# Rows of C for a selective scan: broadcast by DMA through DRAM instead of by matmul and copy

## The chip, the cores and the metric

The kernel runs on one core of one Trainium2 chip. The metric is the time of one execution on the device, in microseconds (us), as the median of several runs.

## The reference

Four layers follow one another on a tensor of 4 images x 64 x 64 pixels x 128 channels. Layers 0, 1 and 3 are vision state space layers, layer 2 is a gated block without a scan. What matters here is the scan of layers 0, 1 and 3, cut to its core:

```
xs = stack([x0, x1, x0 reversed, x1 reversed])   # 4 directions, 256 channels, 4096 positions
dts, Bs, Cs = split(x_proj @ xs, [8, 16, 16])    # per direction
delta = softplus(dt_w @ dts + dt_b)
h = exp(delta * A) * h + (delta * x) * B         # state: 256 channels x 16
y = sum over the 16 states of h * C
```

x1 is x0 with rows and columns of the image exchanged. After the scans the four directions are summed, normalized, multiplied by a gate silu(z), projected, and an MLP with gelu follows. Each layer also has a layernorm and (in the scan layers) a depthwise 3x3 convolution ahead of it.

## The kernel before

**Tiling.** Channels lie on the 128 partitions, 256 channels make two halves h (DH = 2). The 4096 positions are cut into 8 chunks of 512 (CH, NCH). For each of 12 images (3 scan layers x 4) the function `scans` runs the four directions in the order DIRS = (0, 2, 1, 3), and in each the 8 chunks: the first and the last are written out, the six between are three passes of a loop over two chunks. A chunk has N = 16 steps, one for each state n. So there are 12 x 4 x 8 = 384 chunks and 6144 steps, and each step does its work on both halves.

**One step, engine by engine.** Every engine has its own `chunk` function, and all order comes from semaphores.

- TensorE spreads row n of B over the 128 partitions by a bf16 matmul with a selector SEL (`spread`, L349), two steps ahead, into one of two PSUM banks BB. It spreads row n of C the same way, one step ahead, into the one bank CB. It also sums the products h * C of step n - 4 into the PSUM banks YB with a matmul by the identity (`sum_states`, L361; LAG = 4).
- ScalarE copies CB to the readout ring CS in SBUF (L780; RING = 4 slots), computes the decay factors exp(delta * A) of both halves into two PSUM banks DAB (L787), and saves the last column of the state of the step before into CARRY (`save`, L767).
- VectorE multiplies delta * x by B (L567) and runs the recurrence (L584, a tensor_tensor_scan that reads the decay from PSUM), once for each half. The states go to the ring HS (4 slots).
- GpSimd multiplies the state by C (L937), from HS and CS to the ring HC (4 slots).

**Between chunks.** The next chunk is prepared in slots of the present one: PE_SLOTS, ACT_SLOTS, DVE_SLOTS and POOL_SLOTS name the step after which each piece runs. The projection of the next chunk gives a tile RAW (L739) whose rows 0 to 15 are B, 16 to 31 are C and 32 to 39 the step sizes; it is split into three bf16 parts in PARTS. At step MERGE = 4 ScalarE takes the finished sums of the chunk before out of YB (`take_sums`, L771). In directions 1 and 3 (o = 1) it writes them with rows and columns exchanged. TensorE's first `sum_states` of the new chunk waits for it.

**DMA.** The SP queue issues all transfers. In a scan layer it stores the gates silu(z) to DRAM, reads them back into X0 after the second direction (L280), loads the residual after the last chunk (L260), and stores the results. DIAG, the diagonals of the convolution, is a view of the same memory as CS, and TensorE reads it (L428) until the fifth tile of the convolution is done.

Of the kernel before, what the change touches and what calls it, by code (L numbers as in the profile page):

```python
# [34 lines left out]
LAG = 4  # L35

# [45 lines left out]
def program(nc, x_in, consts, sel_in, w0, w1, wg, w3, out):  # L82
    ctx = ExitStack()
    with ctx:
# [9 lines left out]
        gates = nc.dram_tensor("gates", [P, DH, L], F32).ap()  # L94
        sources = [x_in, *hidden]
# [8 lines left out]
        SEL = sb("SEL", [P, 2 * N, P], BF16)  # L104
# [36 lines left out]
        YB, DAB, BB, CB, PB = PS[:, 0:2], PS[:, 2:4], PS[:, 4:6], PS[:, 6], PS[:, 7]  # L141
# [17 lines left out]
        def both(ap):  # L159
# [13 lines left out]
            "b_ready", "c_ready", "decay_ready", "c_copied", "input_ready", "state_ready", "carry_ready",  # L173
# [25 lines left out]
        class Chunk:  # L199


            def __init__(self, img, ki, j):
# [6 lines left out]
                self.turned = img.scan(NCH) + NCH  # L209

# [42 lines left out]
        def _(sp):  # L253
            sp.dma_start(KC[:, :], consts).then_inc(s["consts_loaded"], 16)
            sp.dma_start(SEL[:, :, :], sel_in).then_inc(s["consts_loaded"], 16)
            for layer, (kind, weights, _) in enumerate(layers):
# [10 lines left out]
                def image(b, more):  # L267
# [5 lines left out]
                    else:  # L273
                        for t in range(NCH):
                            sp.wait_ge(s["gate_ready"], img.scan(NCH) + (t + 1))
                            sp.dma_start(gates[:, :, tok(t)], SZT[t % 2]).then_inc(s[f"gate_stored{t % 2}"], 16)
                        for q in range(2):
                            sp.wait_ge(s[f"gate_stored{q}"], (img.scan(NCH // 2) + NCH // 2) * 16)
                        sp.wait_ge(s["y_merged"], img.scan(CHUNKS) + 2 * NCH)
                        sp.dma_start(X0[:, :, :], gates).then_inc(s["gates_loaded"], 16)  # L280
                        sp.wait_ge(s["y_merged"], img.scan(CHUNKS) + CHUNKS)
# [23 lines left out]
        def _(pe):  # L305
# [58 lines left out]
            def chunk(c, prev, nxt, par):  # L364
                for n in range(N):
# [7 lines left out]
                    if n + 1 < N or nxt:  # L373
                        pe.wait_ge(s["c_copied"], st + 1)
                        m = (n + 1) % N
                        spread(CB, N + m, par if n + 1 < N else 1 - par).then_inc(s["c_ready"], 1)
# [15 lines left out]
            for layer, (kind, _, _) in enumerate(layers):  # L392
# [3 lines left out]
                with pe.Fori(0, NB) as b:  # L396
# [4 lines left out]
                    if kind == "scan":  # L401
# [40 lines left out]
                        spread(CB, N, 0).then_inc(s["c_ready"], 1)  # L442
# [95 lines left out]
        def _(dve):  # L538
# [30 lines left out]
            def chunk(c, prev, nxt, par):  # L569
                for n in range(N):  # L570
                    st = c.step + n
                    for h in range(DH):
# [11 lines left out]
                        dve.tensor_tensor_scan(c.run(HS[n % RING][:, h]), c.run(DAB[:, h]), c.run(DBX[n % 2][:, h]),  # L584
# [137 lines left out]
        def _(act):  # L722
# [12 lines left out]
            def prepare(i, par, op, first=False):  # L735

                if op == "raw":
                    act.wait_ge(s["proj_ready"], i + 1)
                    act.activation(RAW[:, :], PB, ACT.Identity, bias=col(K_ROW)).then_inc(s["raw_ready"], 1)  # L739
# [33 lines left out]
            def chunk(c, prev, nxt, par):  # L773
                final = nxt is None or nxt.k != c.k
                for n in range(N):
                    st = c.step + n
                    act.wait_ge(s["c_ready"], st + 1)
                    if prev or n >= RING:
                        act.wait_ge(s["readout_ready"], st - (RING - 1))
# [253 lines left out]
```

## Time and profile before

| | |
|---|---|
| median of 3 runs | 26486.41 us (26484.9 to 26491.68) |
| span of the profiled execution, first to last instruction | 26472.5 us |
| what the median has around that span | 13.9 us |
| VectorE busy | 25249.3 us, 95% |
| TensorE matmul busy | 20800.8 us, 79% |
| GpSimd busy | 16821.7 us, 64% |
| ScalarE busy | 16551.4 us, 63% |
| mean DMA traffic | 8 GB/s |
| mean granted TensorE clock | 0.957 |

A page of the profile lists busy time by engine and by line. Times of single instructions overlap a little where one starts before the write of the last has ended, so the interval from start to start is what a step costs. Idle time of an engine is put down to what released it.

### The profile page before, as it was taken

To read this page: it belongs to the slowest core of one execution; us is meant where nothing else is said; L and a number is where in the kernel's file an instruction comes from. 1 tells how busy PE (TensorE), PEld (TensorE's weight loads), DVE (VectorE), ACT (ScalarE), POOL (GpSimd) and SP (SyncE) were. 2 spreads that over 40 slices of the span, in tenths; PEclk is the share of its full clock that TensorE was granted. 3 is DMA by queue.
4 is the path that set the end of the run, shared out by engine and by line. 5 is a ranking of instruction groups with operands and counts; after the bars stand their busy time and mean duration, and the time that the engine had idled before them with its cause. 6 is when DMAs were issued, how large, how long until landed. Compare 5 with 4: busy or idle time off the path is not lost.

```text
span 26472.5 us, 271753 instructions
## 1 busy us (share of the span) xinstructions
PE 20800.8 (79%) x48516; PEld 8224.1 (31%) x49344; DVE 25249.3 (95%) x28655; ACT 16551.4 (63%) x31677; POOL 16821.7 (64%) x7108
## 2 busy tenths in 40 slices
PE   7778778778777777877877877787778778778777
PEld 3333333333333333333333333333333333333333
DVE  9998998998999899899899899969999998998998
ACT  6665665665666566666566566656666665665665
POOL 5765765775677477577577567707775765775775
PEclk9999999999999999999999999999999999999999
DMA  0000000000000000000000000010000000000000
GB/s 15 7 0 17 7 0 16 0 7 16 1 7 4 16 7 1 16 0 7 16 0 7 10 7 7 0 58 1 7 4 13 7 0 16 0 7 16 1 7 7
DMA packets 53095, 222.41 MB, mean 8 GB/s; under 512 B 4384, under 2 KB 4512, under 8 KB 45600
## 3 DMA queue, kind: packets, MB, share of 16 engines
q1 hardware_dynamic: 51744, 209.22, 2.1%
q14 instruction: 1091, 8.94, 0.1%
q8 instruction: 260, 4.26, 0.1%
HBM read 125.31 MB, written 83.89 MB: 8 GB/s over the span
## 4 chain that ended last, share of the span: by engine, by line
issue 48%; DVE 34%; PE 7%; ACT 7%; DVEq 3%; POOL 0%; DMA 0%; ACTq 0%; another core or an unknown queue 0%; POOLq 0%; SPq 0%
DVE WK L584 21%; DVE WK L567 7%; PE PS L361 3%; DVE WK L561 2%; ACT PS L787 2%; DVE WK L558 2%; PE PS L474 1%; PE PS L487 1%; ACT YP L771 1%; DVEq L577 1%; DVEq L579 1%; DVE X L645 1%; ACT CS L780 1%; ACT WK L762 1%; PE PS L349 1%
## 5 line engine op out<-in xcount | busy, mean ns | idle before, releaser
L937 POOL TENSOR_TENSOR HC<-WK,CS 128x1024 f32<-128x1024 f32 x6144 | 14824.7, 2415 | 7065.8 <-DVE WK L584 5702.7
L584 DVE TENSOR_TENSOR_SCAN WK<-PS,CARRY,WK 128x512 f32<-128x512 f32 x12288 | 15593.2, 1269 | 114.0 <-ACT PS L787 99.5
L787 ACT ACTIVATE PS<-WK,ANEG 128x512 f32<-128x512 f32 x12288 | 8452.0, 691 | 8013.6 <-DVE WK L584 8009.6
L361 PE MATMUL PS<-HC,KC 128*128 128x512 f32 x24576 | 12368.4, 628 | 648.9 <-ACT YP L771 641.3
L567 DVE TENSOR_TENSOR WK<-WK,PS 128x512 f32<-128x512 f32 x12288 | 8055.4, 656 | 46.6 <-DVE WK L584 45.0
L349 PE MATMUL PS<-PARTS,SEL 128*128 128x512 bf16 x11616 | 3727.7, 398 | 4715.8 <-DVE WK L567 4560.8
L361 PEld LDWEIGHTS PS<-HC,KC 128*128 128x128 f32 x24576 | 4849.4, 200 | 5367.6 <-issue 3879.4
L349 PEld LDWEIGHTS PS<-PARTS,SEL 128*128 128x128 bf16 x12288 | 1155.0, 99 | 9761.2 <-DVE WK L567 8332.6
L780 ACT ACTIVATE CS<-PS 128x512 f32<-128x512 f32 x6144 | 3586.9, 584 | 379.2 <-PE PS L349 358.4
L924 POOL TENSOR_TENSOR WK<-WK 128x1024 f32<-128x1024 f32 x384 | 911.4, 2373 | 2416.4 <-DVE WK L555 2416.4
L767 ACT ACTIVATE CARRY<-WK 128x2 f32<-128x2 f32 x5376 | 1012.8, 188 | 0.0
L928 POOL TENSOR_TENSOR WK<-WK 128x1024 f32<-128x1024 f32 x384 | 909.7, 2369 | 1.8
L345 PE MATMUL PS<-RAW,W 9*128 9x512 f32 x1536 | 874.3, 649 | 12.3
L357 PE MATMUL PS<-YP,KC 128*128 (+1 forms) x1152 | 870.2, 884 | 0.0
L645 DVE SCALAR_TENSOR_TENSOR X<-YP,W,X 128x512 f32<-128x512 f32 x1056 | 755.8, 790 | 0.0
L319 PE MATMUL PS<-X,W 128*128 (+1 forms) x1536 | 751.1, 612 | 0.0
L684 DVE SCALAR_TENSOR_TENSOR WK<-PS,W,X 128x512 f32<-128x512 f32 x96 | 72.0, 750 | 570.7 <-PE PS L474 570.7
L561 DVE TENSOR_TENSOR WK<-WK,X 128x1024 f32<-128x1024 f32 x384 | 604.3, 1574 | 0.4
L771 ACT ACTIVATE YP<-PS 128x1024 f32 (+1 forms) x384 | 560.0, 1458 | 70.4 <-PE PS L361 70.4
L754 ACT ACTIVATE WK<-PS 128x512 f32<-128x512 f32 x768 | 444.0, 578 | 76.3 <-PE PS L345 76.3
L555 DVE TENSOR_SCALAR WK<-WK 128x1024 f32<-128x1024 f32 x384 | 489.4, 1275 | 0.0
L428 PE MATMUL PS<-YP,CS 128*128 128x512 f32 x1080 | 477.8, 594 | 0.6
(114 smaller groups left out, 11580.2 us busy)
## 6 DMA issues: line engine op xcount, KB each, us to landing
gates<-WK SPq DMA_DIRECT2D x96, 512.0 KB, 3.0
X<-gates SPq DMA_DIRECT2D x12, 4096.0 KB, 12.8
X<-hidden SPq DMA_DIRECT2D x20, 2048.0 KB, 8.0
hidden<-WK SPq DMA_DIRECT2D x96, 256.0 KB, 2.0
X<-in_x SPq DMA_DIRECT2D x8, 2048.0 KB, 8.8
YP<-hidden SPq DMA_DIRECT2D x4, 2048.0 KB, 9.2
out<-WK SPq DMA_DIRECT2D x32, 256.0 KB, 2.0
W<-w SPq DMA_DIRECT2D x3, 2004.5 KB, 12.4
```

The costliest lines, as they stand in the source:

```text
L349: return pe.matmul(bank, SEL[:, row], PARTS[:, parity], start=True, stop=True)
L361: mm = pe.matmul(YB[:, h], ident, HC[:, slot, h], start=(n == 0), stop=(n == N - 1))
L561: dve.tensor_tensor(DX[par], DELTA[par], nxt.X[:, :, nxt.tokens()], ALU.mult).then_inc(s["dx_ready"], 1)
L567: dve.tensor_tensor(DBX[slot][:, h], DX[par][:, h], BB[:, slot], ALU.mult).then_inc(s["input_ready"], 1)
L584: dve.tensor_tensor_scan(c.run(HS[n % RING][:, h]), c.run(DAB[:, h]), c.run(DBX[n % 2][:, h]), CARRY[:, n, h:h + 1], ALU.mult, ALU.add).th ...
L645: ins = dve.scalar_tensor_tensor(conv, window, w, conv, ALU.mult, ALU.add)
L767: act.activation(CARRY[:, n], source, ACT.Copy).then_inc(s["carry_ready"], 1)
L780: act.activation(CS[:, n % RING], CB, ACT.Copy).then_inc(s["c_copied"], 1)
L787: act.activation(DAB[:, h], DELTA[par][:, h], ACT.Exp, scale=ANEG[:, a:a + 1])\
L924: pool.tensor_tensor(ROUND[par], EXPV, ROUND[par], ALU.subtract).then_inc(s["err_ready"], 1)
L928: pool.tensor_tensor(LOGV, LOGV, ROUND[par], ALU.add).then_inc(s["log1p_ready"], 1)
L937: pool.tensor_tensor(HC[:, n % RING], HS[n % RING], both(CS[:, n % RING]), ALU.mult).then_inc(s["readout_ready"], 1)
```

## The change

C no longer passes through TensorE and ScalarE. Once a chunk's RAW is there, SP stores its rows 16 to 31 to DRAM, eight copies of each (`store_c`). For each step SP loads row n from the eight copies, each read sixteen times, onto the 128 partitions of a slot of CS (`load_c`, 256 KB). The load waits until GpSimd has done the product that last read the slot; the load of step 15 waits for one product more and so speaks for the load of the next chunk's step 0 as well. The store of the next chunk's rows is placed behind the load of step 5. For the first chunk of an image the store waits until the convolution on TensorE has ended, since CS and DIAG share memory.

The PSUM bank that held C becomes a third bank for decay factors, so that ScalarE can be three half steps ahead of VectorE's scan instead of two. The carry is saved two steps late instead of one (SAVE). The selector has half its rows, and the gates are read back into X0 after the last chunk instead of after the second direction, just ahead of the residual's load.

```
+REPS = 8
+SAVE = 2
+STORE = 5
+DECAY_BANKS = (2, 3, 6)
+        c_rows = nc.dram_tensor("c_rows", [2, REPS, N, CH], F32).ap()
-        SEL = sb("SEL", [P, 2 * N, P], BF16)
+        SEL = sb("SEL", [P, N, P], BF16)
-        YB, DAB, BB, CB, PB = PS[:, 0:2], PS[:, 2:4], PS[:, 4:6], PS[:, 6], PS[:, 7]
+        YB, BB, PB = PS[:, 0:2], PS[:, 4:6], PS[:, 7]
+            def c_loads(self, n):
+                return (self.i * (N // RING) + n // RING) * 16
+            def decay_bank(self, n, h):
+                return PS[:, DECAY_BANKS[(DH * n + h) % len(DECAY_BANKS)]]
...
+            def store_c(par):
+                sp.dma_start(c_rows[par].rearrange("r n l -> n r l"),
+                             RAW[N:2 * N, :].rearrange("p (o l) -> p o l", o=1).to_broadcast([N, REPS, CH]))\
+                  .then_inc(s["c_stored"], 16)
+            def load_c(c, n, par):
+                rows = c_rows[par, :, n:n + 1, :].to_broadcast([REPS, P // REPS, CH])
+                sp.dma_start(CS[:, n % RING], rows).then_inc(s[f"c_loaded{n % RING}"], 16)
+            def chunk(c, prev, nxt, par):
+                for n in range(N):
+                    st = c.step + n
+                    if n == 0:
+                        sp.wait_ge(s["c_stored"], (c.i + 1) * 16)
+                    elif prev or n >= RING:
+                        sp.wait_ge(s["readout_ready"], st - (RING - 1) + (nxt is not None and n == N - 1))
+                    load_c(c, n, par)
+                    if nxt and n == STORE:
+                        sp.wait_ge(s["raw_ready"], nxt.i + 1)
+                        store_c(1 - par)
...
+                        sp.wait_ge(s["conv0_ready"], img.scan(CONV_PE) + CONV_PE)
+                        store_c(0)
+                        scans(sp, img, chunk)
                         for q in range(2):
                             sp.wait_ge(s[f"gate_stored{q}"], (img.scan(NCH // 2) + NCH // 2) * 16)
-                        sp.wait_ge(s["y_merged"], img.scan(CHUNKS) + 2 * NCH)
+                        sp.wait_ge(s["y_merged"], img.scan(CHUNKS) + CHUNKS)
                         sp.dma_start(X0[:, :, :], gates).then_inc(s["gates_loaded"], 16)
-                        sp.wait_ge(s["y_merged"], img.scan(CHUNKS) + CHUNKS)
                         load(src, b, XI, "residual_loaded")
...
-                    if n + 1 < N or nxt:
-                        pe.wait_ge(s["c_copied"], st + 1)
-                        m = (n + 1) % N
-                        spread(CB, N + m, par if n + 1 < N else 1 - par).then_inc(s["c_ready"], 1)
...
                 if op == "raw":
                     act.wait_ge(s["proj_ready"], i + 1)
+                    if not first:
+                        act.wait_ge(s["c_stored"], i * 16)
...
-                    act.wait_ge(s["c_ready"], st + 1)
-                    if prev or n >= RING:
-                        act.wait_ge(s["readout_ready"], st - (RING - 1))
-                    act.activation(CS[:, n % RING], CB, ACT.Copy).then_inc(s["c_copied"], 1)
...
-                        if prev or n:
+                        if prev and n == 0:
                             act.wait_ge(s["state_ready"], st * DH + (h - 1))
+                        elif DH * n + h >= len(DECAY_BANKS):
+                            act.wait_ge(s["state_ready"], st * DH + (h + 1 - len(DECAY_BANKS)))
-                        act.activation(DAB[:, h], DELTA[par][:, h], ACT.Exp, scale=ANEG[:, a:a + 1])\
+                        act.activation(c.decay_bank(n, h), DELTA[par][:, h], ACT.Exp, scale=ANEG[:, a:a + 1])\
...
-                    if n:
-                        save(c, n - 1, final)
+                    if n >= SAVE:
+                        save(c, n - SAVE, final)
                     elif prev:
-                        save(prev, N - 1, prev.k != c.k)
+                        save(prev, N + n - SAVE, prev.k != c.k)
...
-                    pool.wait_ge(s["c_copied"], st + 1)
+                    pool.wait_ge(s[f"c_loaded{n % RING}"], c.c_loads(n) + 16)
```

## Rows read from the trace of the kernel before

**Rows 1.** VectorE's groups by line: busy, mean ns; idle before, releasers.

```profile
L584 DVE TENSOR_TENSOR_SCAN WK<-PS,CARRY,WK 128x512 f32<-128x512 f32 x12288 | 15593.2, 1269 | 114.0 <-ACT PS L787 99.5 <-POOL HC L937 11.4
...
L669 DVE SCALAR_TENSOR_TENSOR YP<-YP,W,WK 128x512 f32<-128x512 f32 x192 | 168.5, 915 | 29.2 <-ACT WK L869 29.2
```

**Rows 2.** Who waited for whom: us in total, times, longest us.

```profile
DVE WK L584 <- ACT PS L787: 99.5, 130, 1.0
...
DVE WK L567 <- DVE WK L584: 45.0, 80, 0.8
```

**Rows 3.** First image, directions 0 and 2, then 1 and 3: busy by engine, clock.

```profile
118.00:1090.00 972.00, 747.78 (x1778) 296.71 (x1810) 969.52 (x1072) 627.53 (x1237) 688.43 (x287) 0.95 0.00 1
1140.00:2062.00 922.00, 725.94 (x1670) 282.14 (x1704) 911.32 (x1007) 583.43 (x1147) 643.61 (x270) 0.95 0.00 0
```

**Rows 4.** Timeline of a merge in a chunk of o = 1: start, us.

```profile
4007.58 2.37 POOL L937 TENSOR_TENSOR HC<-WK,CS 128x1024 f32<-128x1024 f32 x1 [1.17 <-DVE WK L584]
...
4011.12 2.36 POOL L937 TENSOR_TENSOR HC<-WK,CS 128x1024 f32<-128x1024 f32 x1 [1.18 <-DVE WK L584]
...
4011.80 1.91 ACT L771 ACTIVATE YP<-PS 128x1024 f32 x1
...
4013.76 3.78 PE L361 MATMUL PS<-HC,KC 128*128 128x512 f32 x4 [2.20 <-ACT YP L771]
...
4016.87 1.27 DVE L584 TENSOR_TENSOR_SCAN WK<-PS,CARRY,WK 128x512 f32<-128x512 f32 x1
...
4018.44 0.60 ACT L780 ACTIVATE CS<-PS 128x512 f32<-128x512 f32 x1 [2.02 <-PE PS L349]
...
4019.75 1.28 DVE L584 TENSOR_TENSOR_SCAN WK<-PS,CARRY,WK 128x512 f32<-128x512 f32 x1 [1.03 <-ACT PS L787]
```

**Rows 5.** ScalarE's groups of the page: decay factors and copy of C.

```profile
L787 ACT ACTIVATE PS<-WK,ANEG 128x512 f32<-128x512 f32 x12288 | 8452.0, 691 | 8013.6 <-DVE WK L584 8009.6
...
L780 ACT ACTIVATE CS<-PS 128x512 f32<-128x512 f32 x6144 | 3586.9, 584 | 379.2 <-PE PS L349 358.4
```

**Rows 6.** DMA issues: KB each, median us to landing.

```profile
gates<-WK SPq DMA_DIRECT2D x96, 512.0 KB, 3.0
X<-gates SPq DMA_DIRECT2D x12, 4096.0 KB, 12.8
...
hidden<-WK SPq DMA_DIRECT2D x96, 256.0 KB, 2.0
X<-in_x SPq DMA_DIRECT2D x8, 2048.0 KB, 8.8
```

**Rows 7.** Busy by engine, clock, DMA share, GB/s while gates come back amid scans.

```profile
1106.00:1119.00 13.00, 12.45 (x27) 5.29 (x29) 12.88 (x15) 9.72 (x20) 7.99 (x5) 0.80 0.80 323
```

**Rows 8.** Groups by line in the same stretch (1106 to 1120 us): busy, mean ns.

```profile
L937 POOL TENSOR_TENSOR HC<-WK,CS 128x1024 f32<-128x1024 f32 x5 | 11.8, 2357 | 6.2 <-PE PS L361 3.9 <-DVE WK L584 2.3
...
L584 DVE TENSOR_TENSOR_SCAN WK<-PS,CARRY,WK 128x512 f32<-128x512 f32 x8 | 10.2, 1273 | 0.1
```

**Rows 9.** Timeline at the end of the first image's scans.

```profile
2058.98 0.39 PE L349 MATMUL PS<-PARTS,SEL 128*128 128x512 bf16 x1 [0.20 <-ACT CS L780]
...
2075.05 0.34 SPq L260 DMA_DIRECT2D X<-in_x  x1
...
2090.40 5.64 DVE L669 SCALAR_TENSOR_TENSOR YP<-YP,W,WK 128x512 f32<-128x512 f32 x2 [2.44 <-ACT WK L869]
```

**Rows 10.** Timeline at the start of the first image's scans.

```profile
100.54 7.89 PE L428 MATMUL PS<-YP,CS 128*128 128x512 f32 x18
...
120.66 2.36 POOL L937 TENSOR_TENSOR HC<-WK,CS 128x1024 f32<-128x1024 f32 x1 [15.95 <-DVE WK L584]
```

**Rows 11.** Busy by engine and granted clock, ahead of a merge and in it.

```profile
4071.00:4131.35 60.35, 46.98 (x115) 18.12 (x115) 60.35 (x68) 38.88 (x78) 42.88 (x19) 1.00 0.00 0
...
4134.90:4142.00 7.10, 5.85 (x8) 2.49 (x9) 6.20 (x8) 5.08 (x10) 2.80 (x2) 0.53 0.00 0
```

More of the change, by code:

```diff
@@ L172, in program @@
             "abs_done", "e_ready", "ln_ready", "round_ready", "err_ready", "log1p_ready", "delta_ready", "dx_ready",
-            "b_ready", "c_ready", "decay_ready", "c_copied", "input_ready", "state_ready", "carry_ready",
+            "b_ready", "decay_ready", "c_stored", "c_loaded0", "c_loaded1", "c_loaded2", "c_loaded3", "input_ready", "state_ready", "carry_ready",
             "readout_ready", "ysum_done", "y_merged",
@@ L254, in _ @@
             sp.dma_start(KC[:, :], consts).then_inc(s["consts_loaded"], 16)
-            sp.dma_start(SEL[:, :, :], sel_in).then_inc(s["consts_loaded"], 16)
+            sp.dma_start(SEL[:, :, :], sel_in[:, 0:N]).then_inc(s["consts_loaded"], 16)
+            def store_c(par):
[16 more added lines that the diff above has]
+                        store_c(1 - par)
             for layer, (kind, weights, _) in enumerate(layers):
@@ L441, in _ @@
                         spread(BB[:, 1], 1, 0).then_inc(s["b_ready"], 1)
-                        spread(CB, N, 0).then_inc(s["c_ready"], 1)
                         pe.wait_ge(s["x_ready"], x + len(X_ORDER))
@@ L583, in chunk @@
                         dve.wait_ge(s["decay_ready"], st * DH + (h + 1))
-                        dve.tensor_tensor_scan(c.run(HS[n % RING][:, h]), c.run(DAB[:, h]), c.run(DBX[n % 2][:, h]),
+                        dve.tensor_tensor_scan(c.run(HS[n % RING][:, h]), c.run(c.decay_bank(n, h)), c.run(DBX[n % 2][:, h]),
                                                CARRY[:, n, h:h + 1], ALU.mult, ALU.add).then_inc(s["state_ready"], 1)
@@ L857, in _ @@
                         act.wait_ge(s["state_ready"], end * DH)
-                        save(Chunk(img, K - 1, NCH - 1), N - 1, True)
+                        for n in range(N - SAVE, N):
+                            save(Chunk(img, K - 1, NCH - 1), n, True)
                         act.wait_ge(s["ysum_done"], end)
```

## The prediction

> **What bounds the kernel now.** I read the busy shares first: VectorE is busy for 95% of the span, the others for 63 to 79%. Then VectorE's groups by line: the recurrence L584 alone holds 15593.2 us, and has only 114.0 us of idle time ahead of its 12288 instructions, 99.5 us of it put down to ScalarE's decay factors [rows 1]. The table of who waited for whom splits that into 130 waits of at most 1.0 us, and adds 45.0 us in 80 waits ahead of L567 [rows 2]. So however much work is taken from TensorE or ScalarE, the scans can gain no more than those waits. ScalarE, for its part, idles 8013.6 us waiting for VectorE ahead of L787 [rows 5]: it is the engine that waits, not the one waited for, nearly everywhere.
>
> Where the 99.5 us lie I read from two long stretches. In directions 0 and 2 VectorE idles 972.00 - 969.52 = 2.5 us, in directions 1 and 3 it idles 922.00 - 911.32 = 10.7 us [rows 3]. What differs is the merge, whose timeline shows the chain of the waits [rows 4]. ScalarE takes the sums at 4011.80, 1.91 us long. TensorE's summing waits for that and starts at 4013.76; its four matmuls take 3.78 us. In TensorE's order the spreads of B and C stand behind them, so ScalarE, whose next item is the copy of C, stands for 2.02 us until 4018.44. Only after the copy come the decay factors, and the scan that should have followed 1.77 us after the one at 4016.87 (a step is 4011.12 - 4007.58 = 3.54 us, so half a step is 1.77) starts at 4019.75. The interval is 2.88 us, 1.11 too long, of which 1.03 shows as idle; the other 0.08 is overlap of one instruction with the next that is lost.
>
> **The change part by part.**
>
> *C leaves TensorE and ScalarE.* Removed: 6144 copies of 584 ns, 3587 us of ScalarE, and as many spreads of at most 0.39 us [rows 9], 2.4 ms of TensorE or less. Both are worth nothing by themselves, because the scan on VectorE covers them [rows 1, 5]. What counts is the chain above. Without the copy ScalarE does not wait for TensorE between the merge and the next decay factors. From 4011.80, if the merge came no earlier, it would have: take the sums 1.91, two factors 1.3, the two preparing activations of that slot about 1.2, next factor 0.7, which ends at about 4017. The scan wants it at 4016.87 + 1.77 = 4018.64. The stall goes with 1.6 us to spare, and a third bank lets ScalarE reach the merge up to half a step earlier. Gain: 99.5 us plus 130 x 0.08 = 10.4 us, together 109.9 us. What is late next? The spread of B for the step after next also stands behind the 3.78 us of summing; it just meets VectorE now, and moves earlier with the merge. GpSimd's product of step 4 waits for the same sums, but VectorE needs it only for the scan of step 8, over 10 us after the merge. So I let nothing replace the stall. Bounds: nothing gained (the next waiter is as late), or 109.9.
>
> *The third decay bank and the late save.* They only loosen waits. The late save keeps its distance to the ring: VectorE rewrites a slot of HS four steps later, the save comes two steps later. 0 us, covered by ScalarE's 8 ms of idle time [rows 5]. Were that cover gone, each of 12288 factors could cost up to 691 ns.
>
> *The end of an image's scans.* There TensorE is late: it works through the sums of the last steps. In step 14 of the last chunk its order held a spread of C that waited for the copy, 0.39 us plus 0.20 of waiting, about 0.43 net [rows 9]. 12 images x 0.43 = 5.2 us gained; bounds 0 and 12 x 0.59 = 7.
>
> *The selector.* 512 KB less ahead of the weights, at 323 GB/s [rows 7]: 1.6 us, once.
>
> *The loads of C.* Added: 6144 transfers of 256 KB, 1.6 GB, or 256 KB in each 3.54 us step, 74 GB/s; 384 stores of 256 KB. Their price has three sides.
>
> Latency. A transfer of 256 KB landed in 2.0 us, one of 512 KB in 3.0 us [rows 6]: 1.0 us fixed and 1.0 us for 256 KB spread over 16 DMA engines. Eight copies in DRAM suggest work for eight engines: 1 + 2 = 3.0 us, and I take that. From below 2.0; from above one engine: 4096 KB in 12.8 us is 20 KB per us and engine, so 13 us. Against that stands the time a load has. It may start when the product that used the slot is done, and is needed four steps later: 4 x 3.54 - 2.36 = 11.8 us. For step 15, with a wait one product later, 3 x 3.54 - 2.36 = 8.3 us. After a merge, when GpSimd works off its backlog without a pause, 3 x 2.36 = 7.1 us. 3.0 us plus an issue of 0.34 us [rows 9] fits all three. Cost 0; gone from about 7 us on.
>
> What stands behind a wait on SP: in the scans nothing but these loads and the store, whose wait for RAW (ready in step 1) is over before the load of step 5 may go. For the first chunk the store waits for the convolution: TensorE's last 18 matmuls end at 100.54 + 7.89 = 108.43; store 2.0, load 3.0 and two issues end at about 114; GpSimd's first product is at 120.66 [rows 10]. Covered with 6 us.
>
> Contention. For 13 us the trace has both at once, 323 GB/s of traffic, over four times what the loads add, and a running scan [rows 7]. The products took 2357 ns, the scan 1273 ns against 1269 [rows 1, 8]. The 4 ns are what scans after a merge also show without traffic (1.28 against 1.27, [rows 4]). I take 0 for it; from above 4 ns x 24576 instructions of L584 and L567 = 98 us.
>
> Instruction fetch. The 45.0 and 11.4 us of small waits [rows 1, 2] look like passes of the loop beginning anew, since nothing that they wait for is late; code comes by DMA, too. The loads keep the 16 engines busy for 256 KB / 323 GB/s = 0.8 us of 3.54, 22%. I take 22% of 45, 10 us, as a loss; bounds 0 and 56 (those waits doubled).
>
> *The gates come back later.* The load of X0 moves from amid the scans to their end, ahead of the residual's. It goes at 2075.05 and takes 12.8 us, to 2087.9 [rows 6, 9]; the first instruction that needs it, L669, runs at 2090.40. Covered by 2.5 us, cost 0. If the two loads shared the DMA engines evenly, it would land after 12.8 + 8.8 = 21.6 us, at 2096.7: 6.3 us late, x 12 = 75 us. The residual is needed after L669 and L673, at least 168.5 / 12 = 14 us after 2090.40, and is there by 2096.7 either way.
>
> **Sum.** - 109.9 - 5.2 - 1.6 + 10 = - 106.7 us. The profiled execution spans 26472.5 us, and the median 26486.4 has 13.9 us around that, which nothing here changes: 26365.8 + 13.9 = 26379.7, so 26380 us.
>
> **Rivals.**
>
> *A. The stall moves on (12%).* B, the ring or the sums are as late as C was. For it: B stands behind the same 3.78 us. Against it: VectorE's wait is for the decay factors and never for TensorE in these scans [rows 1]. Time: 26486 - 7 = 26480.
>
> *B. The traffic or the code fetches cost more (13%).* Fetches at 56 us instead of 10 give 26426, traffic at 98 us gives 26478, both 26524. For it: 1.6 GB that were not there. Against it: [rows 8].
>
> *C. The gates are late (8%).* 26380 + 75 = 26455, if the residual's load takes its share from the first. Against it: both come from one queue, the gates first.
>
> *D. TensorE's clock falls (4%), slower than before.* The granted clock was 1.00 over 60 us of steps, in which TensorE was busy for 46.98 of 60.35 us, and 0.53, mostly the lower level of 1.2 GHz, in and behind the merge where it had waited [rows 11]; there four matmuls of summing took 3.78 us [rows 4]. The change takes away one matmul of the six of a step. Per step at the lower level: 3.78 + 0.53 for B = 4.3 us against 3.54, so if it stayed there, 6144 x 0.76 = 4.7 ms, 31150 us. It decides only where TensorE's work in a chunk exceeds the chunk: at the upper level that is 46.98 / 60.35 = 78% with C, so even so the clock would have to be at the lower level for 28% of the time, where the mean of 0.95 [rows 3] makes it 10%. The Trainium skill ("TensorE: Matmul & The Clock Gate", The HAM clock gate) says that the throttled state is the default and that activity releases it, which speaks against taking matmuls away. By that rule the full loss is the 31150 above; the trace agrees that waits bring the low level, but shows none in steps without them.
>
> *E. C comes late (5%), slower.* At L937, by a load that gets one DMA engine or two instead of eight: 13 us per load against a step of 3.54 makes 26.5 ms + 6144 x 9.46 us = 84.6 ms; with two, 6.4 us per load, 44.1 ms. From 256 KB / 3.54 us = 72 KB per us on, four engines at 20, it decides nothing. The Trainium skill ("DMA: Bandwidth & Descriptors", Why a DMA increments its semaphore by 16 and not by 1) says that a transfer is spread over the largest number up to 16 that divides the outermost sizes of both sides; here these are 8 and 128, so eight engines. By that rule the load takes the 3.0 us of the sum. No row of before has such a shape.
>
> **How the numbers follow.** The forecast has 58%. A measurement of this kernel can tell about 0.2%, 53 us, so faster means under 26433. The forecast, its own range 26350 to 26430 (stall gone; fetches from 0 to 56; the 56 us of small waits halved on the low side), lies there, and so do 8% of B (fetches alone). Within 0.2% are C, 3% of B (traffic alone) and 11% of A. Slower are D, E and 3% of A and B (a stall of more than before, or both costs of B). Faster 0.66, same 0.22, slower 0.12. The range for 8 in 10 leaves out D, E and the edges: 26345 to 26485.
>
> **What would show it.** L780 and half of L349 are gone. The waits of L584 for L787 fall from 99.5 us to under 10. L937 does not wait for a DMA, loads of C land in about 3 us, traffic is about 65 GB/s. L584 stays at 1269 ns, L937 at about 2415. L669 does not wait for gates. The clock stays near 0.95. Wrong would be: a new releaser ahead of L584 or L567 with 100 us or more, or means of VectorE's lines up by 4 ns and more.

## The result and the profile after

The changed kernel takes 26298.9 us (26298.64 to 26300.54, four runs) against 26485.9 us: 187 us less, a ratio of 0.9929 with an interval of 0.9915 to 0.9943. The prediction was 26380, its range 26345 to 26485; the sign was right, the time lies 46 us under the range.

VectorE's groups by line (busy, mean ns, idle before, releasers), to be read beside [rows 1]:

```profile
L618 DVE TENSOR_TENSOR_SCAN WK<-PS,CARRY,WK 128x512 f32<-128x512 f32 x12288 | 15595.9, 1269 | 14.7 <-ACT PS L821 8.5 <-issue 6.2
L601 DVE TENSOR_TENSOR WK<-WK,PS 128x512 f32<-128x512 f32 x12288 | 8059.5, 656 | 5.1 <-DVE WK L618 2.0
...
L595 DVE TENSOR_TENSOR WK<-WK,X 128x1024 f32<-128x1024 f32 x384 | 603.9, 1573 | 0.4
L589 DVE TENSOR_SCALAR WK<-WK 128x1024 f32<-128x1024 f32 x384 | 486.3, 1266 | 0.0
...
L703 DVE SCALAR_TENSOR_TENSOR YP<-YP,W,WK 128x512 f32<-128x512 f32 x192 | 177.3, 962 | 29.2 <-ACT WK L904 29.2
```

The scan is as long as before, 1269 ns, and so is the multiplication, so the traffic slows neither. (A mean of this kind is a weak witness: the same kernel's next profile, `again`, reads 1282 and 668 ns for the two, with the scans still 1.77 us apart from start to start.) L703, outside the scans, reads 962 ns against 915; over the other runs it lies between 900 and 947, and the 9 us in it were not followed up. The scan's idle time falls from 114.0 to 14.7 us, as foreseen. But the idle time ahead of the multiplication falls too, from 46.6 us (45.0 of it the 80 small waits of [rows 2]) to 5.1, and that was not foreseen. L703 still waits for ScalarE alone, so the gates come in time.

The two halves of the first image, beside [rows 3], and the traffic (last column, GB/s):

```profile
118.00:1090.00 972.00, 694.40 (x1554) 258.70 (x1555) 971.02 (x1075) 515.09 (x982) 687.33 (x287) 0.96 0.24 74
1140.00:2062.00 922.00, 673.84 (x1484) 244.57 (x1482) 915.10 (x1011) 478.26 (x910) 649.25 (x271) 0.98 0.24 73
```

The second window still shows 6.9 us of idle time, but only because the scans now end within it: the timeline further below has the sums taken at 2060.48, before the window's end. The granted clock went up from 0.95 to 0.98 there, not down. A merge in a chunk of o = 1 (timeline: start, us), beside [rows 4]:

```profile
4103.53 1.27 DVE L618 TENSOR_TENSOR_SCAN WK<-PS,CARRY,WK 128x512 f32<-128x512 f32 x1
...
4104.84 0.69 ACT L821 ACTIVATE PS<-WK,ANEG 128x512 f32<-128x512 f32 x1 [1.08 <-DVE WK L618]
4105.31 1.27 DVE L618 TENSOR_TENSOR_SCAN WK<-PS,CARRY,WK 128x512 f32<-128x512 f32 x1
...
4105.56 1.91 ACT L807 ACTIVATE YP<-PS 128x1024 f32 x1
...
4107.08 1.27 DVE L618 TENSOR_TENSOR_SCAN WK<-PS,CARRY,WK 128x512 f32<-128x512 f32 x1
...
4107.52 1.98 PE L400 MATMUL PS<-HC,KC 128*128 128x512 f32 x4 [0.64 <-ACT YP L807]
...
4108.38 0.69 ACT L821 ACTIVATE PS<-WK,ANEG 128x512 f32<-128x512 f32 x1 [0.43 <-DVE WK L618]
4108.85 1.27 DVE L618 TENSOR_TENSOR_SCAN WK<-PS,CARRY,WK 128x512 f32<-128x512 f32 x1
```

The last decay factor ahead of the merge starts when the scan of 4103.53 ends, and is wanted only by the scan of 4108.85, with two scans (4105.31 and 4107.08) between them, where two banks leave one: the lead that the third bank gives. The sums are taken half a step sooner in the chunk than before, TensorE waits 0.64 us instead of 2.20, and its four matmuls take 1.98 us at a granted clock of 1.00 in that stretch, the upper level of 2.4 GHz, instead of 3.78 us at 0.50, the lower one. The scans follow one another at 1.77 us throughout.

The end of the first image's scans, beside [rows 9]:

```profile
2060.48 1.88 ACT L807 ACTIVATE YP<-PS 128x1024 f32<-128x1024 f32 x1 [4.97 <-PE PS L400]
...
2062.45 0.34 SPq L320 DMA_DIRECT2D X<-gates  x1
...
2078.59 4.79 DVE L703 SCALAR_TENSOR_TENSOR YP<-YP,W,WK 128x512 f32<-128x512 f32 x2 [2.44 <-ACT WK L904]
```

and the DMA issues (KB each, us to landing):

```profile
c_rows<-RAW SPq DMA_DIRECT2D x384, 256.0 KB, 4.0
gates<-WK SPq DMA_DIRECT2D x96, 512.0 KB, 3.1
X<-gates SPq DMA_DIRECT2D x12, 4096.0 KB, 12.2
...
X<-in_x SPq DMA_DIRECT2D x8, 2048.0 KB, 13.2
```

The gates land at 2062.45 + 12.2 = 2074.7, 3.9 us ahead of their first use. For a load of C the view gives no time to landing; by its packets the last of them ends 3.2 us after the start of the issue, in the median.

**Where the 187 us are.** I took the starts of all 12288 scans from both traces and summed, over the 384 chunks, what each interval has over 1.773 us, by its place in the chunk. Only two places differ by more than 4 us: the interval ahead of the scan of step 6, which the merge hits, and the one from a chunk's last scan to the next chunk's first. The latter is nonzero only where a loop turns, that is, branches back to its start, behind the third and the fifth chunk of a direction, 96 times.

```
us summed                      before   after   gained
merge (ahead of step 6)         114.0     0.0    114.0
turn of a loop                   65.1    21.2     43.9
all else within the scans     23200.6 23198.3      2.3
between images' scans          2847.3  2831.1     16.2
up to the first scan            117.5   119.1     -1.6
behind the last scan            127.9   127.1      0.8
```

These add up to 175.6; the spans differ by 26472.5 - 26296.8 = 175.7. The other 11 us are not in the traces: the profiled execution of the kernel before was a quick one, as the first run below shows.

### The profile page after: what moved, and what is told of

Same layout as the page of the kernel before. It is cut to its first block, busy times and chain, and to the rows that moved or that the text cites. A ratio compares the mean times of both kernels' runs of the same rounds, so it can differ in the third digit from the quotient of the medians.

```text
span 26296.8 us, 249319 instructions
## 1 busy us (share of the span) xinstructions
PE 19441.9 (74%) x43200; PEld 7276.0 (28%) x43200; DVE 25229.6 (96%) x28655; ACT 13823.5 (53%) x25533; POOL 16793.9 (64%) x7108
## 4 chain that ended last, share of the span: by engine, by line
DVE 66%; issue 23%; DVEq 4%; PE 4%; ACT 2%; POOL 0%; DMA 0%; SPq 0%; POOLq 0%; ACTq 0%
DVE WK L618 55%; DVE WK L601 5%; DVE WK L595 2%; DVE WK L592 2%; DVEq L617 2%; PE PS L508 1%; PE PS L521 1%; DVEq L611 1%; DVEq L613 1%; DVE X L679 1%; ACT WK L765 1%; ACT WK L767 1%; PE PS L350 0%; DVE YP L703 0%; DVEq L616 0%
## 5 line engine op out<-in xcount | busy, mean ns | idle before, releaser
L972 POOL TENSOR_TENSOR HC<-WK,CS 128x1024 f32<-128x1024 f32 x6144 | 14801.4, 2409 | 6927.6 <-DVE WK L618 6500.5
L618 DVE TENSOR_TENSOR_SCAN WK<-PS,CARRY,WK 128x512 f32<-128x512 f32 x12288 | 15595.9, 1269 | 14.7 <-ACT PS L821 8.5
L400 PE MATMUL PS<-HC,KC 128*128 128x512 f32 x24576 | 12166.0, 619 | 131.5 <-ACT YP L807 131.5
L388 PE MATMUL PS<-PARTS,SEL 128*128 128x512 bf16 x6144 | 2457.8, 400 | 6429.9 <-DVE WK L601 6413.3
L388 PEld LDWEIGHTS PS<-PARTS,SEL 128*128 128x128 bf16 x6144 | 600.3, 98 | 11387.9 <-DVE WK L601 10647.4
L595 DVE TENSOR_TENSOR WK<-WK,X 128x1024 f32<-128x1024 f32 x384 | 603.9, 1573 | 0.4
L589 DVE TENSOR_SCALAR WK<-WK 128x1024 f32<-128x1024 f32 x384 | 486.3, 1266 | 0.0
L798 ACT ACTIVATE WK<-WK 128x512 f32<-128x512 f32 x768 | 470.0, 613 | 0.0
## 6 DMA issues: line engine op xcount, KB each, us to landing
X<-gates SPq DMA_DIRECT2D x12, 4096.0 KB, 12.2
X<-in_x SPq DMA_DIRECT2D x8, 2048.0 KB, 13.2
```

The source lines that it names most:

```text
L388: return pe.matmul(bank, SEL[:, row], PARTS[:, parity], start=True, stop=True)
L400: mm = pe.matmul(YB[:, h], ident, HC[:, slot, h], start=(n == 0), stop=(n == N - 1))
L595: dve.tensor_tensor(DX[par], DELTA[par], nxt.X[:, :, nxt.tokens()], ALU.mult).then_inc(s["dx_ready"], 1)
L618: dve.tensor_tensor_scan(c.run(HS[n % RING][:, h]), c.run(c.decay_bank(n, h)), c.run(DBX[n % 2][:, h]), CARRY[:, n, h:h + 1], ALU.mult, AL ...
L972: pool.tensor_tensor(HC[:, n % RING], HS[n % RING], both(CS[:, n % RING]), ALU.mult).then_inc(s["readout_ready"], 1)
```

## The experiments

In the expectations, theory S says that the merges gain because ScalarE no longer stands behind TensorE for C, and the turns because of the third bank. "Merge" and "turn" in what was measured are the sums of the table above, taken in the same way from each kernel's trace. A table at the end of this section sets the kernels side by side.

**The change again.** No edit.

> The changed kernel once more, as the mark for the other three. Its median was 26299 us against 26486 us. If the 13.9 us around the span of the profiled execution of the kernel before were fixed, the same would lie around this one; if they were the luck of one execution, the kernel before will show spans some 10 us longer here and both kernels have about 2 us around the span.

26302.8 us (26293.1 to 26307.5), the kernel before 26485.1 (26478.2 to 26489.3), ratio 0.993 (0.9917 to 0.9944). A run of the kernel before with 26485.06 us has a span of 26483.3, the profiled one of this kernel 26303.35 with 26301.5: 1.8 us lie around a span. So the 26472.5 us of the profiled execution before belong to a time of about 26474.3, and some 12 us of my 13.9 were luck. The trace of this run has 21.5 us at the turns and nothing at the merges, as the first one had.

**Two banks.**

```
-DECAY_BANKS = (2, 3, 6)
+DECAY_BANKS = (2, 3)
```

> The change with two decay banks instead of three; the bank that held C lies idle. Theory S (the merges gain because ScalarE no longer stands behind TensorE for C; the loop's turns gain because the third bank makes the decay factor of a chunk's last scan ready half a step sooner, so that VectorE's instruction sequencer is free sooner and its turn of the loop is hidden): no waits at the merges, the small waits at the turns back at 50 to 65 us, 26299 + 44 = 26343 us. Rival L (the turns gain because TensorE's and ScalarE's loops have less in them): the turns stay at 21 us, 26299 us. Rival M (the third bank removes the waits at the merges too): 26413 to 26460 us.

26359.8 us (26353.7 to 26360.9), ratio 0.9952 (0.9939 to 0.9966), 17 us over the 26343 expected. Merge 0.8, turn 75.5, against 50 to 65 expected. So without C in ScalarE's order, two banks do for the merges, and the third is worth 54 us at the turns. Rival L is out, and so is M in the form that the third bank is needed.

**Two banks and the wait; two banks and the copy.** Ahead of each step's decay factors, the first or the second of these:

```
+                    if n + 1 < N or nxt:
+                        act.wait_ge(s["b_ready"], st + 2)
...
+                    act.activation(SPARE[:, :], RAW[:, :], ACT.Copy).then_inc(s["spare_done"], 1)
```

> Two decay banks, and ahead of each step's decay factors ScalarE waits again for TensorE, as it did for C, now for the spread of B that stood in front of C's in TensorE's order. No copy. Theory S: the merges lose their 114 us again and the turns 44 us, 26299 + 158 = 26457 us. Rival W (it was the 584 ns of the copy, not the wait): 26343 us, as with two banks alone.

> Two decay banks, and ScalarE does a copy of 128x512 (RAW to a spare tile) in each step, without waiting for TensorE. Theory S: the 6144 copies are hidden, 26343 us, ScalarE back at 63% busy. Rival W (the work of the copy made the merges late): 26343 + up to 114 = 26457 us.

The wait: 26386.4 us (26382.4 to 26388.8), merge 24.5, turn 77.8. The copy: 26367.1 us (26364.1 to 26371.7), merge 1.2, turn 77.0. That the copy alone is hidden was expected. But the wait alone misses its 26457 us by 71, and neither brings the 114 us back. The wait for TensorE is not by itself what my prediction took it for.

**Two banks with both, and the whole old path.** The first has the two edits above. The second has TensorE's spread as well, into the sixth bank, with the copy out of it; the products still use what the DMA brings:

```
+                    if n + 1 < N or nxt:
+                        pe.wait_ge(s["c_copied"], st + 1)
+                        m = (n + 1) % N
+                        spread(PS[:, 6], m, par if n + 1 < N else 1 - par).then_inc(s["c_ready"], 1)
...
+                    act.wait_ge(s["c_ready"], st + 1)
+                    if prev or n:
+                        act.wait_ge(s["c_copied"], st)
+                    act.activation(SPARE[:, :], PS[:, 6], ACT.Copy).then_inc(s["c_copied"], 1)
```

> Two decay banks with both the wait for TensorE's spread of B and the copy. By now: two banks alone have no waits at the merges, the wait alone brings 25 us back, the copy alone 1 us; three banks hide both together. Theory A (wait, copy and the decay factors add up along ScalarE's order, and 0.5 us of copy in a step is what was missing): 60 to 114 us at the merges, 26360 + 60 to 114 = 26420 to 26474 us. Rival (the copy is always hidden, what is missing is TensorE's own spread of C): 25 us, 26386 us.

> The whole old path beside the new one: two decay banks, TensorE spreads a row into the sixth bank in each step after the spread of B, ScalarE waits for it and copies it to a spare tile, TensorE waits for the copy. The products still use what the DMA brings. So it is the kernel before plus the traffic. If the decomposition is complete: 114 us at the merges, 75 us at the turns, the late end of the images back: 26360 + 114 + 10 = 26484 us, within 10 us of the kernel before plus 10 for the traffic. If anything else in the change helped: lower by that.

With both 26459.0 us (26453.6 to 26466.5), merge 99.8, turn 74.5. The whole path 26491.0 us (26482.5 to 26495.2), merge 123.9, turn 74.2. The waits of the whole path, as in [rows 2]:

```profile
DVE WK L624 <- ACT PS L831: 109.9, 134, 1.1
DVE WK L607 <- DVE WK L624: 44.1, 81, 0.8
```

against 99.5 in 130 and 45.0 in 80. That is the kernel before over again, with 1.6 GB of traffic on top. Its median is 10 us above the one measured beside it (26480.6), which the interval does not tell from nothing (ratio 1.0004, 0.9995 to 1.0013). Wait and copy add up along ScalarE's order: 24.5 + 1.2 alone, 99.8 together. The other 24 us of the 123.9 come with TensorE's own spread of C and its wait for the copy.

**Three banks and the chain.** The same wait and copy, with three banks.

> The change with three decay banks, but with both the wait for TensorE and a 128x512 copy put back ahead of each step's decay factors. Theory S: the turns stay hidden; at the merges ScalarE can start at most the 0.69 us earlier that it idled ahead of its last factor, so of 1.11 us per wait some 0.4 stay: 30 to 50 us, 26330 to 26350 us. If the third bank does nothing at the merges: 26299 + 114 = 26413 us. If it does everything: 26299 us.

26296.8 us (26294.6 to 26304.9), ratio 0.9932 (0.9919 to 0.9946): the time of the change itself. Merge 0.2, turn 20.2, with ScalarE at 64% busy again.

So beside this wait and this copy the third bank brings by itself all that the change brings in the scans: 99.8 us of merges go to 0.2, 74.5 us of turns to 20.2. Whether it would also absorb the old path with TensorE's spread of C in it, 123.9 us, is not shown; there is no bank left for both. Theory S falls for the merges: what I had argued to 30 to 50 us is 0.

**Late factors in the last step.** Three banks; in step 15 the factors wait as with two:

```
-                        if prev and n == 0:
+                        if (prev and n == 0) or n == N - 1:
```

> The change as it is, three banks, but in step 15 the decay factors wait as if there were two. Only the scans ahead of the turn of a loop are touched. Theory S: the waits at the turns come back, 50 to 65 us in all, 26299 + 44 = 26343 us, with no wait at the merges. Rival L (leaner loops): 26299 us.

26346.5 us (26342.5 to 26349.5), ratio 0.9951 (0.9937 to 0.9964). Merge 0.0, turn 75.6. The waits of the turns are back, 80 and at eight of them a second one, and nothing else:

```profile
DVE WK L601 <- DVE WK L618: 45.6, 80, 0.8
DVE WK L618 <- issue: 21.2, 8, 2.8
```

One such turn in its timeline (VectorE, then ScalarE):

```profile
6771.03 1.27 DVE L618 TENSOR_TENSOR_SCAN WK<-PS,CARRY,WK 128x512 f32<-128x512 f32 x1
6772.80 0.69 DVE L601 TENSOR_TENSOR WK<-WK,PS 128x512 f32<-128x512 f32 x1 [0.50 <-DVE WK L618]
...
6768.79 0.69 ACT L821 ACTIVATE PS<-WK,ANEG 128x512 f32<-128x512 f32 x1 [2.60 <-DVE WK L618]
```

The scan at 6771.03 is the last ahead of the turn. Its factor is done at 6768.79 + 0.69 = 6769.48, and only then can VectorE's sequencer, the part that reads the instructions and sends them to the engine, send it and go on to the turn. The first instruction behind the turn starts at 6772.80, 3.3 us later. It was wanted at 6771.03 + 1.19 = 6772.22. The trace has the sequencer's own instructions too, the branch (duration in ns, then start) and the first one behind it:

```profile
L254 DVEq COMPARE_BRANCH  x1: 63/63/63, 6769.7 to 6769.7; - x1
L254 DVEq FUSED_REGOPS  x1: 204/204/204, 6772.5 to 6772.5; - x1
```

So the branch passes 0.26 us after the factor is done, and then the sequencer stands for 2.7 us. In that stretch, 6769.7 to 6772.5, all DMA queues together moved one packet, of 8 KB, in a queue marked as that of instructions:

```profile
DMA packets 1, 0.01 MB, mean 3 GB/s; under 512 B 0, under 2 KB 0, under 8 KB 0
q14 instruction: 1, 0.01, 1.0%
```

It starts at 6770.69. I counted this over all 96 turns of the kernel. At 80 the sequencer stands for 2.7 to 3.0 us, and each has exactly one such packet, 0.93 to 1.26 us behind the branch. At the other 16, one direction of the first layer and one of the second, it goes on after 0.25 us, there is no packet, and the turn costs nothing. The changed kernel has the same 80 and 16. So the price of a turn is the wait for code.

In the changed kernel the same factor was done over 4 us ahead (ScalarE waited 4.25 us before its next one, 6756.9 to 6761.15), the branch passes at 6759.7, 1.9 us ahead of the last scan's start, and the turn does not show:

```profile
6761.61 1.27 DVE L618 TENSOR_TENSOR_SCAN WK<-PS,CARRY,WK 128x512 f32<-128x512 f32 x1
6762.81 0.66 DVE L601 TENSOR_TENSOR WK<-WK,PS 128x512 f32<-128x512 f32 x1
...
6761.15 0.69 ACT L821 ACTIVATE PS<-WK,ANEG 128x512 f32<-128x512 f32 x1 [4.25 <-DVE WK L618]
```

**The traffic.** Without loads (SP's chunk loop replaced by four loads per image, the products wait for those alone), also with two banks, and with each load twice:

```
-                        scans(sp, img, chunk)
+                        sp.wait_ge(s["c_stored"], (img.scan(1) + 1) * 16)
+                        for n in range(RING):
+                            load_c(None, n, 0)
...
+                    sp.dma_start(SPARE[:, n % 2], c_rows[par, :, n:n + 1, :].to_broadcast([REPS, P // REPS, CH]))\
+                      .then_inc(s[f"spare{n % RING}"], 16)
```

> Leaves out the loads of C but for the first four of each image, and the stores but for the first, so that the products use the rows of the first chunk. It measures what 1.6 GB of traffic, the waits for it and SP's code cost the change. My prediction had 10 us for it; expected: 26285 to 26299 us, VectorE's means the same. A rival in which traffic slows VectorE or GpSimd: 26250 us or less.

> Two decay banks and no loads of C but the first four of each image (the products use the rows of the first chunk, so part of the work is left out). Theory F (code fetched at the turns shares the DMA engines with the loads, and two banks leave no time to hide it): the turns cost 65 us as in the kernel before instead of 75, 26350 us. Rival (the 10 us at the turns come from SP's waits or from the placement of the code): 75 us, 26360 us.

> Each row of C is loaded twice, the second time into a spare tile that nobody reads: about 145 GB/s instead of 73. If traffic costs nothing: 26299 us. If each GB/s had a price: twice what the run without loads gains.

Without loads 26292.6 us (26290.5 to 26295.8), merge 0.0, turn 17.0; with two banks 26341.8 us (26339.4 to 26344.6), turn 62.4 against 75.5 with the loads. With twice the traffic 26507.4 us (26501.4 to 26518.3), ratio 1.0011 (1.0002 to 1.0020): slower than the kernel before, where the expectation had at most twice the 6 us that the run without loads gains. The merge is still at 0.0, the scan at 1271 ns, and GpSimd's product has the mean that it has in the change, 2409 ns; it waits for no DMA here either. Of the 209 us over the change 204 are at the turns, 225.6 in the sum:

```profile
L625 DVE TENSOR_TENSOR_SCAN WK<-PS,CARRY,WK 128x512 f32<-128x512 f32 x12288 | 15610.4, 1271 | 23.3 <-issue 23.3
L608 DVE TENSOR_TENSOR WK<-WK,PS 128x512 f32<-128x512 f32 x12288 | 8075.6, 657 | 196.2 <-issue 194.1 <-DVE WK L625 0.4
```

The same turn as above:

```profile
6802.84 1.27 DVE L625 TENSOR_TENSOR_SCAN WK<-PS,CARRY,WK 128x512 f32<-128x512 f32 x1
6806.83 0.69 DVE L608 TENSOR_TENSOR WK<-WK,PS 128x512 f32<-128x512 f32 x1 [2.72 <-issue]
```

The scan before the last had started at 6801.07, so the one before that ended near 6800.6 and let the sequencer go on; the turn is over at 6806.83, some 6.2 us later. The branch passes at 6800.93, but the packet of code starts only at 6804.58, 3.65 us behind it instead of 0.95, amid a stretch (6801 to 6806.5) in which the loads take half of the DMA engines' time:

```profile
q1 hardware_dynamic: 468, 0.90, 50.5%
q14 instruction: 1, 0.01, 0.4%
```

Over the 72 turns that have such a packet outside the last direction of the last layer it starts 3.4 us behind the branch in the median (2.3 to 4.6); in the kernels with 73 GB/s and in those without loads it is 0.93 to 0.95. So traffic makes the turns dear by delaying the packet of code. In the changed kernel a turn has 3.47 us from the last wait to the moment at which its first instruction is wanted, and the 3.4 us that most turns take just fit; at 142 GB/s they no longer do.

The 13 us between two banks with and without loads are not spread over the turns. The excess at the turns, split (us; the other 16 turns have 0.0 in each kernel, and parts can differ by 0.6 from the sums above, which take in all ends of chunks):

```
                     72 turns   8 turns of the last
                                direction, last layer
before                  48.0          17.2
two_banks               48.1          27.9
two_banks_no_loads      45.9          16.6
after                    5.5          15.7
no_loads                 4.7          12.4
double_traffic         184.1          41.6
```

At those eight a second packet of code follows the first, and the first scan behind the turn waits for it. It starts 2.4 to 2.8 us behind the first one in the kernel before and without loads, and 3.7 to 3.8 us behind it with two banks and the loads; in the changed kernel two of the eight come so late, by over 4 us. That is where most of the 10 us of traffic are; the 72 others hardly feel it until it is doubled.

**Slots moved**, a version suggested by L589 and L595 in the profile after:

```
-DVE_SLOTS = {(8, 0): "round", (13, 1): "delta", (14, 0): "input"}
+DVE_SLOTS = {(8, 1): "round", (13, 1): "delta", (14, 1): "input"}
```

> The change with two pieces of VectorE's preparation placed half a step later: round behind the second scan of step 8 and input behind the second scan of step 14. In the trace round takes 1.28 us amid scans and 0.67 us at its fastest, input 1.58 against 1.22; both stand behind the first scan of a step, while GpSimd's product of the step before still runs. Theory P (they are held up by GpSimd's product, and behind the second scan GpSimd is idle): 384 x (0.6 + 0.35) = 365 us less, 25935 us. Rival (GpSimd's next product starts at the same moment and gets ahead of them): no gain, or up to 2.36 us per piece lost, 26300 us and up.

26056.2 us (26052.0 to 26057.3), ratio 0.9839 (0.9826 to 0.9853): 243 us under the change, 424 us under the kernel before. Round is where the gain was expected; input half gives it back:

```profile
L601 DVE TENSOR_TENSOR WK<-WK,PS 128x512 f32<-128x512 f32 x12288 | 8108.8, 660 | 92.0 <-DVE WK L595 81.2 <-DVE WK L618 7.7
...
L595 DVE TENSOR_TENSOR WK<-WK,X 128x1024 f32<-128x1024 f32 x384 | 459.6, 1197 | 0.4
...
L589 DVE TENSOR_SCALAR WK<-WK 128x1024 f32<-128x1024 f32 x384 | 255.3, 665 | 0.0
```

Round fell from 1266 to 665 ns, 231 us. Input fell from 1573 to 1197 ns, 144 us, but now the next multiplication, which reads its result, stands right behind it and waits, 81.2 us; the lost overlap takes more, and the intervals around input fall by 32 us in all. The turns rise from 21 to 39: the branch now passes 2.9 us before the first instruction behind the turn is wanted, instead of 3.1. In the change, round starts at 1120.06, while a product of GpSimd runs from 1118.44 to 1120.79; moved, it starts at 1110.72 and GpSimd's product at 1110.88:

```profile
1118.44 2.35 POOL L972 TENSOR_TENSOR HC<-WK,CS 128x1024 f32<-128x1024 f32 x1 [1.19 <-DVE WK L618]
...
1120.06 1.28 DVE L589 TENSOR_SCALAR WK<-WK 128x1024 f32<-128x1024 f32 x1
```

```profile
1110.72 0.67 DVE L589 TENSOR_SCALAR WK<-WK 128x1024 f32<-128x1024 f32 x1
...
1110.88 2.71 POOL L972 TENSOR_TENSOR HC<-WK,CS 128x1024 f32<-128x1024 f32 x1 [1.19 <-DVE WK L618]
```

The one that starts second pays: VectorE in the first, GpSimd, whose product takes 2.71 instead of 2.35, in the second. The Trainium skill ("SBUF — State Buffer", Who interferes with whom) says that VectorE in a two-port mode, which a tensor_scalar can enter, or with two SBUF inputs contends with GpSimd for a shared pair of ports, and that whoever issues first holds the pair while the other waits. The traces agree: 1.28 us against 0.67 for VectorE, 2.71 against 2.35 for GpSimd.

All kernels by what they have (us; merge and turn as summed above):

```
                      banks  C's chain on ScalarE  traffic  time     merge  turn
before                  2    spread, wait, copy      no     26485.9  114.0   65.1
two_banks_full_chain    2    spread, wait, copy      yes    26491.0  123.9   74.2
two_banks_both          2    wait, copy              yes    26459.0   99.8   74.5
two_banks_wait          2    wait                    yes    26386.4   24.5   77.8
two_banks_copy          2    copy                    yes    26367.1    1.2   77.0
two_banks               2    none                    yes    26359.8    0.8   75.5
two_banks_no_loads      2    none                    no     26341.8    0.9   62.4
late_last_decay         3*   none                    yes    26346.5    0.0   75.6
three_banks_chain       3    wait, copy              yes    26296.8    0.2   20.2
after                   3    none                    yes    26298.9    0.0   21.2
no_loads                3    none                    no     26292.6    0.0   17.0
double_traffic          3    none                    twice  26507.4    0.0  225.6
* two in step 15
```

## Why the prediction was wrong, and where it was right

**The bound was right for this change.** VectorE's 1.77 us per half step is the same in every kernel here, and of the scans' time the change could have only the waits. `slots_moved` shows that there was more to be had from the pieces between them.

**The merges: the size was right (109.9 against 114.0), the cause half right.** The chain that I read, from the sums over TensorE's matmuls to the copy, exists, but it has two remedies. Without wait and copy two banks leave 0.8 us; with wait and copy, though not with TensorE's spread of C, three banks leave 0.2. I credited the first and put the second at nothing.

**The step that failed: "The third decay bank and the late save. They only loosen waits. ... 0 us"** and, with it, the sign of the term of the small waits. I had read the 45.0 + 11.4 us as the turns of the loops, which they are (80 of the 96 turns, and the second wait at eight of them). But in the sum I took them as fixed, with only a loss by traffic to come, 10 us with bounds from 0 to 56; only the low edge of the range let them halve, and no cause was given for that. They hang on when VectorE's sequencer gets to the branch, and that hangs on the decay factor of the chunk's last scan, which the third bank brings half a step sooner. The term measured -43.9 us: -54 by the bank (75.5 to 21.2), about +10 by the traffic (65.1 to between 74 and 78 with two banks). The late save is in every kernel here but the one before, so what it does by itself is not shown.

That the loss by traffic came out at 10 us was luck. I had 22% of all small waits. Those of the 72 turns did not grow (48.0 and 48.1 us); the 10 us are the second packets of eight turns (17.2 to 27.9), and with the third bank the loads cost only 4 us at the turns (17.0 to 21.2). The error of this step is 54 of the 80 us between 26380 and 26299.

**The base.** I put 13.9 us around the span where 1.8 are, and so made the sum from a quick execution; 11 us more came off the median than off the profiled span. A range that must hold a median has to allow for where the one profiled execution lies in the spread of the others, 26469 to 26491 us here.

**The end of the images.** 0.81 us each instead of 0.43, 9.7 us in all, measured from the last scan to the taking of the sums. More left TensorE's order there than the 0.43 us that I had taken for the spread of C and its wait; what the rest is was not followed up. The other 6.5 us between the scans lie in stretches that the change does not touch; most of them is one place, VectorE's additions of the projection up to the first result, which takes either 28.3 or 30.0 us in both kernels, and I have not looked for its cause.

**The selector.** Half the size, but the first scan comes 1.6 us later, not sooner: the weights let VectorE go at 16.46 instead of 15.91. The rest of the delay was not followed up.

**Loads, gates, start, contention: right.** GpSimd's products never wait for a DMA, and their mean is 2409 ns against 2415. A load's last packet ends after 3.2 us, where I had 3.0. The gates land 3.9 us ahead in the first image. At 73 GB/s neither VectorE's scan and multiplication nor GpSimd's product is longer than without the loads.

**The rivals.** A did not happen, not even with two banks (merge 0.8), where the sums are taken no sooner than before; so B's spread was never as late as C's copy. B (fetches) is real, at 4 us in the change and some 10 with two banks, and double the traffic shows how steep it gets. C did not happen: the gates took 12.2 us, and the residual behind them 13.2, so sharing did not hold up the gates. D went the other way: the mean granted clock rose from 0.957 to 0.968, and with two banks it was 0.949. In the one merge shown above TensorE waits less and its matmuls run at the upper level; that this makes the whole rise was not tried. D's arithmetic has a slip: 28% is the share of TensorE's work that would have to run at the lower level for its work of 78% to fill a chunk, and at half the clock that is 44% of the time, not 28%. E did not happen.

## What to carry to other kernels

A buffer between two engines gives lead not only to the work but also to the consumer's instruction sequencer, which can go on to a loop's turn only when its last wait is over. A deeper buffer where the producer idles anyway can hide that turn. Here it did more (26296.8 us with wait and copy still in place) than taking the work away did (26359.8 us with two banks). A small wait that recurs at a loop's turns is not a constant: ask which wait the sequencer stood at before it, and look for the branch and the packet of code behind it. Before adding steady DMA traffic to a kernel with loops, look at what the turns have to spare.

## What the runs showed of the hardware

- Where a turn of VectorE's loop needs code, it takes 3.3 us from the end of the last wait ahead of it to the first instruction behind it, in the median of late_last_decay, of the kernel before and of two banks with and without loads; 2.7 us of it lie between the branch and the sequencer's next instruction. At 142 GB/s it takes 6.0 us in the median (4.9 to 7.4), while the durations of the instructions do not change.
- The code comes as a packet of 8 KB in an instruction queue: in late_last_decay and in the change, one at each of the 80 turns at which the sequencer stands, none at the 16 where it goes on after 0.25 us. The trace does not name the engine that a packet is for; that it is VectorE's is inferred from its place, 0.93 to 1.26 us behind VectorE's branch each time.
- The turns do not cost the same everywhere. In all kernels here, those of one direction of the first layer and one of the second cost nothing, and those of the last direction of the last layer cost most (2.0 to 2.4 us each in the kernel before), because a second packet follows. So it is a matter of the place in the program; which property of the place was not tried.
- A VectorE instruction on two SBUF operands, or a tensor_scalar on SBUF alone, is up to 0.6 us longer beside a running GpSimd product (665 to 1266 ns, 1197 to 1573 ns), and in the one case shown the product is 0.36 us longer when it comes second.
